# Softmax attention rebuilt inside a large kernel: fp32r operands in row tiles, exponentials 1024 wide, maxima in a ring of three PSUM banks

## What is computed

```
h = _layernorm(x, ln1_g, ln1_b)              # Bb = 1, Ss = 4096, H = 16 heads, Dh = 16
q = (h @ Wq).reshape(Bb, Ss, H, Dh)          # k, v alike
scores = jnp.einsum('bqhd,bkhd->bhqk', q, k) / jnp.sqrt(jnp.float32(Dh))
attn = jax.nn.softmax(scores, axis=-1)
ctx = jnp.einsum('bhqk,bkhd->bqhd', attn, v).reshape(Bb, Ss, Dd)
x = x + ctx @ Wo
```

## Time and profile before

| | |
|---|---|
| median of 3 runs | 4788.13 us (4787.18 to 4795.99) |
| the profiled execution | 4786.92 us |
| its span | 4785.1 us |
| PE busy | 4246.9 us (89%), 22137 instructions |
| ACT busy | 3712.3 us (78%), 6966 |
| DVE busy | 3629.5 us (76%), 7272 |
| POOL busy | 2070.0 us (43%), 1034 |
| PE weight loads | 1694.7 us (35%) |

### The profile page before, as it was taken

The page is one execution under the profiler, slowest core; times in us unless marked ns, Lnnn a source line. Parts: engine busy times, 40 slices in busy tenths (PEclk is TensorE's granted clock), DMA queues, the critical chain, the costliest instruction groups (busy, mean ns, idle before and its releaser), DMA issues. The chain is left out here.

```text
span 4785.1 us, 96158 instructions
## 1 busy us (share of the span) xinstructions
PE 4246.9 (89%) x22137; PEld 1694.7 (35%) x22137; DVE 3629.5 (76%) x7272; ACT 3712.3 (78%) x6966; POOL 2070.0 (43%) x1034
## 2 busy tenths in 40 slices
PE   7569999999999999999999999999999962499991
PEld 4322222222222222222222222222222242499990
DVE  3558898889899888988898998889898852133335
ACT  1347999999999999999999999999999841255550
POOL 0011343434344343434343443434343513788875
PEclk8777999999999999999999999999999985799995
DMA  2231010101001010101001010101010023344433
GB/s 78 101 83 17 0 17 0 17 0 17 12 5 17 0 17 0 17 0 17 4 13 17 0 17 0 17 0 17 0 17 0 0 88 108 118 137 138 139 113 114
DMA packets 105459, 176.11 MB, mean 37 GB/s; under 512 B 16512, under 2 KB 87552, under 8 KB 99072
## 3 DMA queue, kind: packets, MB, share of 16 engines
q1 hardware_dynamic: 86864, 146.17, 11.8%
q0 software_dynamic: 6336, 16.79, 1.1%
q10 hardware_dynamic: 12144, 12.06, 0.7%
HBM read 117.55 MB, written 57.15 MB: 37 GB/s over the span
## 5 line engine op out<-in xcount | busy, mean ns | idle before, releaser
L741 ACT ACTIVATE probs<-s_ps 128x512 f32<-128x512 f32 x4096 | 2427.1, 600 | 211.4 <-PE s_ps L683 159.3
L590 POOL TENSOR_TENSOR probs_low<-probs 128x1024 f16<-128x1024 f32 x640 | 1325.1, 2071 | 2081.0 <-ACT probs L741 2081.0
L804 DVE TENSOR_TENSOR probs_low<-probs 128x1024 f16<-128x1024 f32 x1408 | 1819.2, 1294 | 20.8 <-ACT probs L741 20.6
L797 DVE CUSTOM_DVE_ANT_0 excess<-b_ps,excess 128x512 f32<-128x512 f32 x2048 | 1400.7, 686 | 332.2 <-ACT excess L728 268.0
L683 PE MATMUL s_ps<-q_ring,k_ring 98*128 (+1 forms) x4096 | 1564.4, 384 | 13.6 <-ACT probs L741 8.3
L728 ACT ACTIVATE excess<-diff_ps 128x512 f32<-128x512 f32 x2048 | 1214.5, 593 | 58.9 <-PE diff_ps L627 51.5
L666 PE MATMUL o_ps<-probs,v_parts 128*64 128x512 bf16 x4106 | 853.5, 412 | 74.7 <-ACT o_here L733 72.2
L627 PE MATMUL diff_ps<-kd_ring,q_ring 96*128 (+1 forms) x2048 | 804.0, 393 | 50.3 <-issue 38.5
L683 PEld LDWEIGHTS s_ps<-q_ring,k_ring 98*128 98x128 bf16 x4096 | 434.7, 106 | 1158.5 <-ACT probs L741 569.6
L636 PE MATMUL b_ps<-k_ring,q_ring 96*128 (+1 forms) x2048 | 800.6, 391 | 10.0 <-DVE unit_max L797 9.2
L666 PE MATMUL o_ps<-probs_low,v_parts 128*64 128x512 f16 x4106 | 783.2, 377 | 0.0
(11 more groups left out here) (199 smaller groups left out, 3455.2 us busy)
## 6 DMA issues: line engine op xcount, KB each, us to landing
w_in<-in_W SPq DMA_DIRECT2D x46, 1024.0 KB, 4.9
q_ring<-qs_dram SPq DMA_DIRECT2D x96, 128.0 KB, 4.4
k_ring<-ks_dram SPq DMA_DIRECT2D x96, 128.0 KB, 7.0
slots_dram<-zero_rows SPq DMA_DIRECT2D x24, 512.0 KB, 6.5
rows_e<-slots_dram SPq DMA_DIRECT2D x24, 512.0 KB, 3.9
y_slots_dram<-y_out ACTq DMA_DIRECT2D x23, 512.0 KB, 4.2
qs_dram<-parts SPq DMA_DIRECT2D x16, 384.0 KB, 2.9
ks_dram<-parts SPq DMA_DIRECT2D x16, 384.0 KB, 4.1
```

Source lines behind the costliest of these rows:

```text
L590: nc.gpsimd.tensor_tensor(probs_low[:, t % BUFS, :, :], probs[:, t % BUFS, :, :], high[:, :, :, 1], ALU.subtract).then_inc(pool_low_done, 1)
L741: nc.scalar.activation(probs[:, t % BUFS, k, :], s2_ps[:, k, :], ACT.Exp).then_inc(exp_done, 1)
L797: nc.vector.tensor_tensor_reduce(excess[:, u % 2, :], b_ps[:, u % 2, :], excess[:, u % 2, :], 1.0, LEAST, ALU.add, ALU.max, unit_max[:, u ...
L804: nc.vector.tensor_tensor(probs_low[:, t % BUFS, :, :], probs[:, t % BUFS, :, :], high[:, :, :, 1], ALU.subtract).then_inc(low_done, 1)
```

## The change

**Operands.** q and k are cut into two pieces in fp32r, of three products: 48 rows and 2 for the maximum. `k_ring` and `q_stage` hold them twice, from partition 0 and from partition 64 (`TOP_ROW`): the lower copy of `k_ring` has one half of the keys, the upper the other. A pair is two matmuls, one in rows 0 to 49 and one in rows 64 to 113. `q_stage` has four buffers of one chunk, loaded by `load_q`.

**A chunk** has 16 pairs of scores (2 x 128 keys x 512 queries into two banks), with one exponential 1024 wide each (`probs` has room for the whole chunk), and 16 pairs of maxima for the chunk two ahead (`LEAD`). 11 of these pairs are two plain maxima on DVE straight from PSUM, 5 (`RELU_PAIRS`) go as before over a difference, ACT and DVE. All of them go through `m_ps`, three single banks in a ring of 33 blocks a chunk; the 33rd is the turned output.

**Values.** Units 3, 6, 9, 12, 15 (`FULL_UNITS`) are no longer split: their `probs` go to PE in fp32 against `v_full`. The other 11 are split, all on POOL. PE takes them in 11 visits behind certain slots (`VISITS`, `SLOTS`; a slot from 16 up lies in the next chunk).

**The row of maxima.** DVE finishes a chunk's maximum in four instructions behind slots 1, 4, 7 and 10 of the next chunk's units (`finish_max`), the turn being DVE's own transpose in blocks of 32. SP's `rows` then issues 2 copies x 2 pieces x 4 blocks = 16 DMAs of 4 partitions each for the next chunk, and PE waits for all of them (`rows_in`) ahead of a chunk's first score.

**Output.** PE turns `o_ps` with one fp32 matmul, DVE copies it to `ctx_stage`, SP stores sums and outputs in DRAM, and `output_projection` loads them, spreads 1/sum over the heads with PE (`spread`) and multiplies on DVE (`scale`).

The core of the diff:

```diff
-
-Q_PARTS = (0, 0, 0, 1, 1, 2)
-K_PARTS = (0, 1, 2, 0, 1, 0)
+
+PARTS = 2
+Q_PARTS = (0, 0, 1)
+K_PARTS = (0, 1, 0)
 SROWS = len(Q_PARTS) * DH
 MROWS = 2
 AROWS = SROWS + MROWS
...
+TOP_ROW = 64
...
-STEP = 2 * P
-STEPS = TOKENS // STEP
-KCH = TOKENS // CHUNK // 2
-UNITS = TPC * KCH
...
+SIDE = TOKENS // 2
+UNITS = SIDE // P
+KCH = SIDE // CHUNK
+PAIR = 2 * CHUNKS
+RING = HEADS * CHUNKS
+Q_BUFS = 4
+LEAD = 2
+SQ = 32
 LEAST = -3.4e38
-LAG = 5
-BUFS = 8
-POOL_SPLITS = tuple(t for t in range(STEPS) if (t + 1) * 5 // STEPS > t * 5 // STEPS)
-DVE_SPLITS = tuple(t for t in range(STEPS) if t not in POOL_SPLITS)
-RING = HEADS * CHUNKS
+HEAD_DMAS = 16 * 3 * len(K_PARTS)
+Q_DMAS = 16 * 2 * len(Q_PARTS)
+ROW_DMAS = 16 * 2 * MROWS * (P // SQ)
+
+FULL_UNITS = (3, 6, 9, 12, 15)
+POOL_UNITS = tuple(t for t in range(UNITS) if t not in FULL_UNITS)
+VISITS = ((0, 1), (3,), (2, 4), (6,), (5, 7), (9,), (8, 10), (12,), (11, 13), (15,), (14,))
+SLOTS = (11, 13, 14, 15, 16, 17, 19, 20, 21, 22, 24)
+COPY_SLOT, TURN_SLOT = 8, 12
+RELU_PAIRS = (1, 4, 7, 10, 14)
+FINISH_SLOTS = (1, 4, 7, 10)
+RING_BLOCKS = 2 * UNITS + 1
+TURN_BLOCK = 2 * TURN_SLOT + 2
+SPLIT_OPS = 5 + len(FULL_UNITS)
+
...
-            def rows(n):
-
-                col = sp.snap(((n + 15) & 15) * CHUNK)
-                sp.wait_ge(rows_made, n + 2)
-                sp.sem_inc(sync_passed, 1)
-                for r in range(MROWS):
-                    sp.dma_start(q_ring[SROWS + r:SROWS + r + 1, ds(col, CHUNK)].rearrange("a (t n) -> a t n", t=TPC),
-                                 max_parts[:, r, :]).then_inc(row_in, 16)
-                sp.wait_ge(row_in, n * (MROWS * 16) + MROWS * 16)
...
+            def rows(n, buf):
+                sp.wait_ge(max_ready, n + 1)
+                for at in (0, TOP_ROW):
+                    for r in range(MROWS):
+                        row = q_stage[at + SROWS + r:at + SROWS + r + 1, ds(buf * CHUNK, CHUNK)].bitcast(F32)
+                        row = row.rearrange("a (t b n) -> a t b n", t=TPC, b=P // SQ)
+                        for b in range(P // SQ):
+                            sp.dma_start(row[:, :, b, :], max_turned[SQ * b:SQ * b + TPC, r, :]).then_inc(rows_in, 16)
+
...
+                sp.wait_ge(m_read, n * RING_BLOCKS + ((LEAD + 1) * RING_BLOCKS + TURN_BLOCK + 1))
+                sp.dma_start(dram["ctx"][ds(qc, 1), ds(h, 1), :, :].rearrange("a b c x -> (a b c) x"),
+                             ctx_stage[0:DH, b, :]).then_inc(ctx_out[b], 16)
+                sp.dma_start(dram["z"][ds(h * CHUNKS + qc, 1), :], ctx_stage[DH:O_COLS, b, :]).then_inc(ctx_out[b], 16)
+
+            sp.wait_ge(ones_set, 1)
...
+            def chunk(h, qc, loads=True, more=True, ahead=True, before=True):
+
+                i = sp.snap(h * CHUNKS + qc)
+                if loads:
+                    sp.wait_ge(s_done, i * UNITS + 1)
+                    n = qc + LEAD + 1
+                    load_q(sp.snap(h + n // CHUNKS), n % CHUNKS, n % Q_BUFS)
+                    if more and qc == 0:
+                        load_head(sp.snap(h + 1), sp.snap((h + 1) & 1))
+                if ahead:
+                    rows(i + 1, (qc + 1) % Q_BUFS)
+                if before:
+                    store(i - 1, 1 - qc % 2, sp.snap(h - 1) if qc == 0 else h, (qc - 1) % CHUNKS)
...
-                    high = probs[:, t % BUFS, :, :].bitcast(BF16).rearrange("p k (n two) -> p k n two", two=2)
-                    pool.wait_ge(exp_done, i * (2 * STEPS) + (2 * t + 4))
-                    pool.sem_inc(pool_passed, 1)
-                    nc.gpsimd.tensor_tensor(probs_low[:, t % BUFS, :, :], probs[:, t % BUFS, :, :], high[:, :, :, 1],
-                                            ALU.subtract).then_inc(pool_low_done, 1)
-
...
+            def max_pair(it, c, t):
+
+                par, buf = c % PAIR // CHUNKS, c % Q_BUFS
+                col = buf * CHUNK + P * (t // KCH)
+                key = CHUNK * (t % KCH)
+                for k, at in enumerate((0, TOP_ROW)):
+                    b = block_of(t, k)
+                    if c * RING_BLOCKS + b > 2:
+                        pe.wait_ge(m_read, it * (PAIR * RING_BLOCKS) + (c * RING_BLOCKS + b - 2))
+                    ring = kd_ring if k == 0 and t in RELU_PAIRS else k_ring
+                    nc.tensor.matmul(m_ps[:, b % 3, :], q_stage[at:at + SROWS, col:col + P],
+                                     ring[at:at + SROWS, par, key:key + CHUNK], start=True, stop=True).then_inc(m_done, 1)
+
...
+            def scores(it, c, t):
+                par, buf = c % PAIR // CHUNKS, c % Q_BUFS
+                if c * UNITS + t > 1:
+                    pe.wait_ge(exp_done, it * (PAIR * UNITS) + (c * UNITS + t - 1))
+                for k, at in enumerate((0, TOP_ROW)):
+                    last = nc.tensor.matmul(s_ps[:, t % 2, k, :], k_ring[at:at + AROWS, par, P * t:P * t + P],
+                                            q_stage[at:at + AROWS, buf * CHUNK:buf * CHUNK + CHUNK], start=True, stop=True)
+                last.then_inc(s_done, 1)
+
+            def values(it, c, visit):
+
...
+                        pe.wait_ge(pool_low_done, i * len(POOL_UNITS) + (POOL_UNITS.index(t) + 1))
+                    first, final = t == VISITS[0][0], t == VISITS[-1][-1]
+                    if t in FULL_UNITS:
+                        for k in range(2):
+                            last = nc.tensor.matmul(o_ps[V_COLS * k:V_COLS * k + V_COLS, :],
+                                                    v_full[:, par, FULL_UNITS.index(t), k, :], probs[:, t, k, :],
+                                                    start=False, stop=False)
+                        continue
+                    for n, part in enumerate((high_view[:, t, :, :, 1], probs_low[:, POOL_UNITS.index(t), :, :])):
+                        for k in range(2):
+                            last = nc.tensor.matmul(o_ps[V_COLS * k:V_COLS * k + V_COLS, :],
+                                                    v_parts[:, par, first_tile(t) + 2 * k, :], part[:, k, :],
+                                                    start=(first and n == 0), stop=(final and n == 1))
                 last.then_inc(pv_done, 1)
 
-            def step(i, head, par, par_before, qc, ahead):
...
+            def turn_o(it, c):
+
+                pe.wait_ge(o_copied, it * PAIR + c)
+                pe.wait_ge(m_read, it * (PAIR * RING_BLOCKS) + ((c + LEAD) * RING_BLOCKS + TURN_BLOCK - 2))
+                nc.tensor.matmul(m_ps[:, TURN_BLOCK % 3, :], gather[:, :], o_here[:, :], start=True, stop=True
+                                 ).then_inc(o_turned, 1)
...
+            def chunk(it, c, ahead):
...
-            pe.wait_ge(start_values, 4)
...
-                nc.tensor.matmul(o_ps[V_COLS * k:V_COLS * k + V_COLS, :], v_parts[:, 1, 0, :], probs_low[:, 0, 0, :],
-                                 start=True, stop=False)
...
-            for t in range(-LAG, 0):
-                values(pe.snap(RING), 1, t)
-            for t in range(TPC):
-                turn_o(RING, t)
+                        max_pair(it, c + LEAD, t)
+                    for visit, slot in enumerate(SLOTS):
+                        if slot == t:
+                            values(it, c, visit)
+                        if slot == t + UNITS and c > 0:
+                            values(it, c - 1, visit)
+                    if t == TURN_SLOT and c > 0:
+                        turn_o(it, c)
...
+            def excess_pair(n, t):
+
+                act.wait_ge(m_done, n * (2 * UNITS) + (2 * t + 1))
+                nc.scalar.activation(excess[:, :], m_ps[:, block_of(t, 0) % 3, :], ACT.Relu).then_inc(excess_ready, 1)
...
+            def chunk(i, ahead, first=False):
+                for t in range(UNITS):
+                    if ahead and t in RELU_PAIRS:
+                        excess_pair(i + LEAD, t)
+                    act.wait_ge(s_done, i * UNITS + (t + 1))
+                    if not first:
+                        act.wait_ge(pv_done, i * len(VISITS) + (visit_of(t) + 1 - len(VISITS)))
+                    nc.scalar.activation(probs[:, t, :, :], s_ps[:, t % 2, :, :], ACT.Exp).then_inc(exp_done, 1)
+                    if t == COPY_SLOT and not first:
+                        copy_o(i)
...
+            def pair(n, t, b, skip):
+
+                qt, j = t // KCH, t % KCH
+                if t in RELU_PAIRS:
+                    dve.wait_ge(excess_ready, n * len(RELU_PAIRS) + (RELU_PAIRS.index(t) + 1))
+                    dve.wait_ge(m_done, n * (2 * UNITS) + (2 * t + 2))
+                    dve.sem_inc(dve_passed, 1)
+                    nc.vector.tensor_tensor_reduce(excess[:, :], m_ps[:, block_of(t, 1) % 3, :], excess[:, :], 1.0, LEAST,
+                                                   ALU.add, ALU.max, unit_max[:, b, qt, 2 * j:2 * j + 1]
+                                                   ).then_inc(m_read, 2)
+                    return
+                for k in range(2):
```

(52 more changed lines are left out.)

609 lines of the change are left out of this document (262 added, 347 removed).

## The result

The change makes the kernel slower: 5227.2 us (5225.44 to 5244.15, 4 runs) against 4788.93 (4 runs), a ratio of 1.0919 with a 95% interval of 1.0904 to 1.0933. The forecast was 5075, slower, with a range of 4480 to 5750.

What follows compares the result with a forecast made beforehand. ScalarE was taken to bound the kernel (24.0 of 26.7 us a chunk), PE close behind. 128 x 29.7 - 3434.8 - 79 = +288 us on 4786.9 gave 5075 us, range 4480 to 5750.

Steps and rivals of the forecast that it cites:

- The row chain: At a chunk's end, PE's next scores wait for 16 row DMAs issued behind slot 10; period 28 to 33 us, chance 0.52.
- the likeliest case: The 128 chunks wait for their rows of maxima: period 29.7 us, 4860 to 5500 us in all, chance 0.52.
- 17.0 + 12.7 = 29.7: Period of a chunk in us: 17.0 to the end of slot 10, then 12.7 for row DMAs, landing and hand-offs.
- The signs that the prediction named: In the profile after: exponential near 1.06 us, split near 1.9, paired scores, first-score waits of 4 to 6 us, 127 times.
- the ring: Three PSUM banks for maxima: a Relu pair frees its two after 1.83 us, stalling PE 0.3 or 1.35 us each time.
- the last rival: PE far slower in the chunks, as pairs don't run together or the clock falls: 5330 to 6650 us, chance 0.16.
- The time to slot 10: From a chunk's start to the end of slot 10: 17.0 us, of which PE's own work is 12.6.
- PE's walk: PE's pass through a chunk: 20.3 us of work, a period of 24.4 us with stalls but no wait for rows.
- Without this wait it would be 24.4: Period of a chunk if PE did not wait for the row DMAs: 12.6 + 2.45 + 1.35 + 8.0 = 24.4 us.
- the faster rival: The rows of maxima arrive in time: period 24.4 us, 4396 us in all (4102 at 22.1), chance 0.30.
- the row's 0.08: In PE's matmuls, each change of tile form costs 0.08 us, read from a profile row, instead of a full drain.
- The clock: PE's clock falls after idle stretches: 2 to 4 us more a period, 5330 to 5590 us; within a rival of chance 0.16.

Runs made afterwards that it cites:

- e1: The change with the four finishing instructions of a chunk's maximum behind slots 0, 1, 2, 3 instead of 1, 4, 7, 10: 5078.2 us.
- e2: The change with the last finishing instruction of a chunk's maximum behind slot 13 instead of slot 10: 6480.4 us.
- e4: The change with minus the maximum kept in one row instead of two, so 8 row DMAs instead of 16: 5110.0 us.

## Why the prediction was right, and where it was off

**The row chain** was the likeliest case, at 28 to 33 us a period and 4860 to 5500 us, and the measured 30.64 and 5227 lie in it. Forecast 17.0 + 12.7 = 29.7; an undisturbed chunk has 18.4 + 10.0 + 1.15 = 29.56. The two terms were off in opposite ways, 1.4 us too few and 1.55 too many, and that the sum came out within 0.2 us is luck. A row DMA takes 0.573 us on SP and the next starts 0.62 after it, not 0.73: the spacing of the earlier trace rows was between two DMAs with instructions between them that the new stream doesn't have. The sentence from the Trainium skill (DMA: Bandwidth & Descriptors, Why a DMA increments its semaphore by 16 and not by 1) fits the sizes, 0.57 for a copy from 4 rows and 0.45 for those from 16 (six in 2.69), but no run changed that number alone.

The signs that the prediction named are mixed. The wide exponential, the split and the score pairs are as foretold. PE's wait at a chunk's first score was to be 4 to 6 us, 127 times: it is 2.35 in the undisturbed chunk, and 38.3 us in all, in 24 chunks. The waits for `unit_max` (196.9 and 23.4 us), by which the ring would bound, are larger, and the clock of 0.83 is under the 0.9 of the last rival. What shows the chain is e1, e2 and e4, not these signs. And it is worth less than foretold: 2.4 us a period over the walk in an undisturbed chunk, for 29.7 - 24.4 = 5.3, and 149 us when e1 takes it away.

**The time to slot 10** was 1.4 us short. A Relu pair holds its banks 2.05 us and not 1.83, since the Relu ends at 2421.14 and VectorE starts at 2421.41, a hand-off of 0.27, where I had 0.05 for each. And an fp32 unit's visit costs 1.01 + 0.21 for the tile form, 1.22, not 1.04.

**PE's walk** is the term of the sum that was mis-sized most. "Without this wait it would be 24.4": e1_early took the wait away, and the walk is 27.13. Had the rows been in time, as in the faster rival, the kernel would still have been slower than before: that rival's 4396 us was not to be had by any speed of the DMAs. PE's bare work is 16 x 0.46 + 5 x 1.20 + 5 x 1.22 + 0.77 + 1.26 = 21.5. The 5.6 us that are left I put down to waits for VectorE's maxima, where I had 4.1 above 20.3. The pairs of matmuls in row tiles do run together, 0.23 apart, as I had assumed from column tiles. By the rule of the Trainium skill that I had weighed (TensorEngine Tiling (Array Packing), Key Properties) a change of form drains the array; each change costs 0.1 (0.34 for 0.23 between scores and maxima), so the row's 0.08 was the better number.

**The clock** was put wholly into another rival, at 0.16, as if it either happened or not. It happened on top: 30.64 - 29.5 = 1.1 us a period, 145 us, which is nearly all of 5227 - 5075. That I took a lower level after idle stretches from the earlier trace rows and then let the sum of the likeliest case, which has 5 us of idle time a chunk, do without it, is the step that failed.

**Ahead and behind the chunks**: up to the first score -66 was forecast (-61 and -5) and -58 measured, for the projection -8 and -11.

**Why the change doesn't gain.** It takes ScalarE and VectorE down to 18 or 19 us a chunk, but leaves PE a walk of 27.1 us for 26.7 before, then the row chain over that (+2.4), then the clock (+1.1). These parts hold in this order only: with the chain gone (e1) the clock costs 2.4, since less of it is hidden. Three edits undo this: finish the maximum in slots 0 to 3, drop the Relu pairs (VectorE has room for 32 plain maxima), and one visit behind each slot. With them the same design takes 4412.4 us, ratio 0.9193 (0.9171 to 0.9216) to the kernel before.
